# A four-layer graph and expert network: the first twelve expert slabs placed beside the last routing, a second table for the others, expert weights folded two by two, input variances on ScalarE

## The reference

```python
x = x + gnn0(layernorm(x), adj)      # 2-layer attention-like mixing with exp weights, per graph
x = x + ffn0(layernorm(x))           # 30 iterations: h += 0.01 tanh(h); silu; layernorm; h @ W + b
x = x + relu(f @ Gw[:128] + (adj @ f) @ Gw[128:] + bias),  f = layernorm(x)
# experts: 8 of them, the best 2 for each token
logits = xt @ Wr + br;  p = softmax(logits);  top_p, top_idx = top_k(p, 2);  w = top_p / sum(top_p)
xn = layernorm(xt)                                   # over 128 channels
h = gelu((xn * ln_g[e] + ln_b[e]) @ W1[e] + b1[e])   # 128 -> 512
y = h @ W2[e] + b2[e]                                # 512 -> 128
x = x + sum of w * y over the two chosen experts
```

## Time and profile before

| | |
|---|---|
| median of 3 runs | 2514.82 us |
| profiled execution | 2515.02 us, its span 2513.2 us |
| TensorE busy | 2373.5 us, 94% |
| VectorE busy | 2086.3 us, 83% |
| ScalarE busy | 1866.4 us, 74% |
| GpSimd busy | 2024.6 us, 81% |
| mean granted TensorE clock | 0.976 of 2.4 GHz |

### The profile page before, as it was taken

How to read it: one execution, slowest core, us unless ns; L and a number is a source line. 1 busy time by engine, 2 the same in 40 slices (tenths; PEclk the granted TensorE clock), 3 DMA queues, 4 the chain that set the end, 5 groups by cost and what they waited for, 6 DMA issues and landing times.

```text
span 2513.2 us, 61190 instructions
## 1 busy us (share of the span) xinstructions
PE 2373.5 (94%) x19694; PEld 2310.1 (92%) x19951; DVE 2086.3 (83%) x5808; ACT 1866.4 (74%) x2280; POOL 2024.6 (81%) x1733
## 2 busy tenths in 40 slices
PE   6929999999999999999999999999994999999998
PEld 6829999999999999999999999989973999999998
DVE  7999999999999999999999999998983444444443
ACT  3879999999999999999999999946531333333333
POOL 5879999999999999999999999995765444444444
PEclk9969999999999999999999999999986999999999
DMA  9200000000000000000000000011323655555554
GB/s 252 84 0 1 0 0 0 0 0 0 0 0 0 0 0 0 0 0 0 0 0 0 0 0 0 0 32 60 104 82 117 215 215 212 212 213 214 210 211 149
DMA packets 124120, 162.43 MB, mean 65 GB/s; under 512 B 14526, under 2 KB 77146, under 8 KB 124032
## 3 DMA queue, kind: packets, MB, share of 16 engines
q1 hardware_dynamic: 113792, 141.64, 16.9%
q0 software_dynamic: 9088, 17.14, 2.0%
q10 hardware_dynamic: 1152, 2.62, 0.3%
HBM read 36.35 MB, written 24.58 MB: 24 GB/s over the span
## 4 chain that ended last, share of the span: by engine, by line
DVE 59%; PE 31%; issue 6%; ACT 2%; POOL 1%; DMA 1%; SPq 0%; DVEq 0%; POOLq 0%; ACTq 0%
DVE pair_stats L605 26%; DVE state L689 20%; PE psum L1287 11%; PE psum L1296 11%; DVE state L670 7%; PE psum L1119 4%; PE psum L1109 2%; DVE it_vars L609 2%; DVE x_stats L605 1%; POOL sorted_rows L555 1%; ACT state L984 1%; PE psum L1246 1%; PE psum L1277 1%; DVE resid L716 1%; DVE state L685 1%
## 5 line engine op out<-in xcount | busy, mean ns | idle before, releaser
L1119 PEld LDWEIGHTS psum<-w_ffn,turned 128*128 128x128 f32 x7680 | 1009.4, 192 | 36.0
L1119 PE MATMUL psum<-w_ffn,turned 128*128 128x128 f32 x7680 | 1012.9, 275 | 12.8 <-issue 0.2
L510 POOL TENSOR_TENSOR it_rstd<-it_vars,minus_half 128x8 f32<-128x8 f32 x480 | 785.5, 1637 | 0.0
L513 POOL TENSOR_TENSOR state<-state,it_rstd 128x768 f32<-128x768 f32 x480 | 708.2, 1475 | 37.6
L605 DVE BATCH_NORM_STATS2 pair_stats<-state 128x6 f32<-128x256 f32 x1920 | 684.9, 416 | 0.0
L1109 PE MATMUL psum<-ident,state 128*128 128x128 f32 x4352 | 595.1, 280 | 55.9 <-DVE state L685 44.4
L689 DVE SCALAR_TENSOR_TENSOR state<-state,psum 128x1024 f32<-128x1024 f32 x464 | 560.3, 1208 | 0.2
L1109 PEld LDWEIGHTS psum<-ident,state 128*128 128x128 f32 x4352 | 476.3, 142 | 74.3 <-issue 56.7
L969 ACT COPY turned<-psum 128x1024 f32<-128x1024 f32 x480 | 485.8, 1012 | 78.4 <-PE psum L1109 40.8
L979 ACT ACTIVATE state<-state 128x1024 f32<-128x1024 f32 x480 | 512.8, 1068 | 29.3 <-DVE state L685 9.1
L976 ACT ACTIVATE state<-psum 128x1024 f32<-128x1024 f32 x464 | 480.9, 1036 | 0.0
(11 more groups left out here) (207 smaller groups left out, 1829.5 us busy)
## 6 DMA issues: line engine op xcount, KB each, us to landing
adjT<-resid SPq DMA_DIRECT2D x304, 320.0 KB, 2.4
adjT<-sorted_rows SPq DMA_DIRECT2D x156, 66.5 KB, 1.9
resid<-in_x_dram SPq DMA_DIRECT2D x16, 512.0 KB, 7.3
state<-in_adj_dram SPq DMA_DIRECT2D x16, 512.0 KB, 7.3
adjT_dram<-adjT SPq DMA_DIRECT2D x7, 512.0 KB, 4.9
adjT<-adjT_dram SPq DMA_DIRECT2D x7, 512.0 KB, 3.5
adjT<-resid ACTq DMA_DIRECT2D x8, 320.0 KB, 2.7
out_dram<-resid,store_at POOLq DMA_INDIRECT x156, 2.7
```

The source lines that it names most:

```text
L510: nc.gpsimd.tensor_tensor(it_rstd[s % 8][:, :], it_vars[s % 4][:, :], minus_half[:, 0:TILES], ALU.pow).then_inc(it_pow, 1)
L513: nc.gpsimd.tensor_tensor(values[s][:, 0:POOL_TILES, :], values[s][:, 0:POOL_TILES, :], wide(it_rstd[s % 8][:, 0:POOL_TILES]), ALU.mult).t ...
L1119: last = nc.tensor.matmul(dst[:, t, :], stationary(t), moving(t), start=bias is None and m == 0, stop=m == len(terms) - 1, skip_group_chec ...
```

## The change

- **Input variances.** In the last pass the sixteen variances of the input (L609 there) leave VectorE; ScalarE computes them as `x2_variance` with an Identity activation, scale 1/128 and a bias tile `offset`.
- **Folding.** The gain is put into the matrix as a diagonal: ScalarE builds `fold_mats` (ident times the gain plus the offset term), TensorE's product gives the whole folded matrix, ScalarE copies it back. Two experts are folded in each of slots 11 to 14, one ahead of the logits and one behind the ranks. The expert weights are loaded two by two, from the fifth stream on.
- **Twelve slabs first.** After six streams (EARLY = 5) at least 12 slabs are full whatever the input: (6 · 1024 - 28 · 127) / 128 = 20. At the end of slot 12 VectorE computes a table of these (`first_slabs`), in slot 14 it writes it (`first_table`). SyncE loads their rows from slot 14 on and their weights behind the folding, GpSimd scales all twelve with four instructions behind stream 9's scatters (`scale_first`). They have output tiles of their own (`y_first`), since their stores come only after the last scatter.
- **Loops shortened.** VectorE's slot loop ends with slot 18, TensorE's and ScalarE's with 19. What was left for the slots after is written out between the first slabs.
- **The others' table** is computed behind slabs 0 and 1, spread in two parts while TensorE is at slabs 4 and 5, and written behind slabs 3 and 4. Slabs 12 to 155 come out of it. The first round of twelve drains (`end=True`), and the turns of slabs 12 and 13 stand behind it.

```diff
+    EARLY = 5
...
-        FOLD_FROM = STREAMS - 3
+        FOLD_FROM = 11
+        TABLE_FROM = EARLY + PLACE_LAG
...
+            sp.wait_ge(tables_ready, 1)
+            for h in range(2):
+                sp.wait_ge(scattered[h], 16 * (EARLY + 1) * TILES // 2)
+            sp.wait_ge(mix_psum, 13)
+            for n in range(FIRST_ROWS):
+                load_rows(n)
+            second_weights(2)
+            sp.wait_ge(w1_scaled, NE)
+            sp.wait_ge(pads_b2_in, 16 * 3)
+            for n in range(2):
+                load_weights(n)
+            sp.wait_ge(x3_ready, 13)
+            second_weights(4)
+            for n in range(FIRST_ROWS, EACH):
+                load_rows(n)
+            sp.wait_ge(x3_ready, 14)
+            second_weights(6)
+            for n in range(2, 4):
+                load_weights(n)
+            for n in range(4, EACH):
+                load_weights(n)
             AHEAD = 3
-            sp.wait_ge(tables_ready, 1)
-            sp.wait_ge(pads_in, 16 * 2)
+            sp.wait_ge(tables_ready, 2)
+            load_weights(EACH)
             for h in range(2):
                 sp.wait_ge(scattered[h], 16 * STREAMS * TILES // 2)
-            for n in range(4 + AHEAD):
+            for n in range(EACH, EACH + AHEAD + 1):
                 load_rows(n)
...
+                if m == 9:
+                    for rows in row_groups:
+                        scale_first(rows, 0 if rows is row_groups[0] else FIRST_ROWS)
...
             for n in range(6):
-                scale(n)
-            for n in range(SLABS):
+                scale(EACH + n)
+                store(2 * n)
+                store(2 * n + 1)
+            for n in range(EACH, SLABS):
...
                         dve.wait_ge(x2_ready, k + 1)
+                        if k >= 4:
+                            dve.wait_ge(x2_var_ready, k - 3)
                         statistics(x1_stats[k % 4], resid[k]).then_inc(x2_stats_done, 1)
-                        dve.wait_ge(x2_stats_done, k + 1)
-                        variance(x_var[k], x1_stats[k % 4]).then_inc(x2_var_ready, 1)
...
+            def first_slab(o):
+                if o + 4 < EACH:
+                    normalize(0, o + 4)
+                finish(0, o)
+            last = STREAMS - 1
+            normalize(0, 0)
+            normalize(0, 1)
+            scale_logits(last - 1)
+            find_slots(last - 3)
+            route(last - 1)
+            rows_roots(last)
+            normalize(0, 2)
+            scale_logits(last)
+            find_slots(last - 2)
+            normalize(0, 3)
+            best(last, 0)
+            best(last, 1)
+            choose(last)
+            find_slots(last - 1)
+            find_slots(last)
+            first_slab(0)
+            other_slabs()
+            first_slab(1)
+            other_rows()
+            first_slab(2)
+            first_slab(3)
+            other_table(0)
+            first_slab(4)
+            other_table(1)
+            for o in range(5, EACH - 1):
+                first_slab(o)
...
+            def x2_variance(s):
+                act.wait_ge(x2_stats_done, s + 1)
+                nc.scalar.activation(halves(x_var[s]), of_stats(x1_stats[s % 4], 2), ACT.Identity, bias=offset[:, 0:1],
+                                     scale=1.0 / D).then_inc(x2_var_ready, 1)
...
+            def fold_matrix(e):
+                nc.scalar.activation(fold_mats[:, e, :], ident[:, :], ACT.Identity, bias=fold[:, e:e + 1],
+                                     scale=params[:, e, 0:1]).then_inc(fold_ready, 1)
+            def folded(e):
+                act.wait_ge(fold_psum, e + 1)
+                nc.scalar.copy(w1_all[:, e, 0:H], psW).then_inc(w1_scaled, 1)
...
-                if 0 <= k - FOLD_FROM < NE:
-                    fold_sums(k - FOLD_FROM)
+                if 0 <= k - FOLD_FROM < NE // 2:
+                    fold_sums(2 * (k - FOLD_FROM))
...
+                    ranks(h)
+                if 0 <= k - FOLD_FROM < NE // 2:
+                    fold_sums(2 * (k - FOLD_FROM) + 1)
...
+                    if first and o == 1:
+                        ranks(STREAMS - 2)
+                    if first and o == 3:
+                        ranks(STREAMS - 1)
+                    if first and o == 9:
+                        spread(psT[0], diag[0], "other")
+                    if first and o == 11:
+                        spread(psT[1], diag[1], "half")
```

More of the change, by code:

```diff
@@ new lines, in _, with count_slabs, sum_up @@
+            steps = pair_steps[:, 1, :]
+            def count_slabs(offset):
+                table(nc.vector.tensor_tensor(steps, pair_end[:, :], region_0[:, :], ALU.subtract))
+                table(nc.vector.tensor_scalar(steps, steps, 1.0 / SLAB, offset, ALU.mult, ALU.add))
+                table(nc.vector.tensor_scalar(steps, steps, float(1 << 23), None, ALU.add))
+            def sum_up():
+                reach, at = 1, 0
+                while reach < PAIRS:
+                    old, new = slab_ends[at], slab_ends[1 - at]
+                    table(nc.vector.tensor_tensor(new[:, LEAD:], old[:, LEAD:], old[:, LEAD - reach:LEAD + PAIRS - reach],
+                                                  ALU.add))
+                    reach, at = 2 * reach, 1 - at
+                assert at == 1
@@ L892, in _ @@
-            table(nc.vector.tensor_tensor(past[:, :, :], ends.unsqueeze(1).to_broadcast([P, 2, PAIRS]),
-                                          slab_j[:, :].unsqueeze(2).to_broadcast([P, 2, PAIRS]), ALU.is_le))
-            for h in range(2):
-                last = nc.vector.tensor_tensor(past_steps[:, h, :, :], pair_steps[:, :, :],
-                                               past[:, h, :].unsqueeze(1).to_broadcast([P, 5, PAIRS]), ALU.mult)
-            table(last)
-            table(nc.vector.tensor_reduce(slab_is[:, :, :], past_steps[:, :, :, :], AX.X, ALU.add))
@@ L944, in finish, with experts @@
                 last.then_inc(y_ready, 1)
-            def experts(i, first=False, end=False):
+            def first_slab(o):
[29 more added lines that the diff above has]
+                first_slab(o)
+            def experts(i, end=False):
                 for o in range(EACH):
@@ L950, in experts @@
                         normalize(i, o + 3)
-                    if not first or o >= 1:
-                        finish(i, o - 1, not first or o >= 5)
+                    finish(i, o - 1)
             for n in range(3):
-                normalize(0, n)
-            experts(0, first=True)
+                normalize(0, EACH + n)
             with dve.Fori(1, SLABS // EACH - 1, 1) as i:
@@ L1083, in experts @@
                     gelu(i, 2 * o + 1)
+                    if o in between:
+                        weights_exp(between[o])
             for n in range(2):
                 turn(0, n)
-            experts(0)
+            experts(0, end=True, between={0: STREAMS - 2, 1: STREAMS - 1})
+            for n in range(2):
+                turn(0, EACH + n)
             with act.Fori(1, SLABS // EACH - 1, 1) as i:
@@ L1311, in _ @@
             pe.wait_ge(experts_in[1], 16 * NE)
-            experts(0, first=True)
+            experts(0, first=True, end=True)
+            pe.wait_ge(tables_ready, 2)
+            for n in range(2):
+                turn(0, EACH + n)
             with pe.Fori(1, SLABS // EACH - 1, 1) as i:
```

402 lines of the change are left out of this document (250 added, 152 removed).

## The result

The changed kernel has a median of 2495.27 us over 4 runs (2492.36 to 2501.0); the kernel before, beside it, 2514.71 (4 runs, 2514.58 to 2514.89). The ratio is 0.9927 [0.9915, 0.994]: 19.4 us faster, where 27.5 were forecast. It spreads more than the kernel before, and its time goes with the mean granted clock of TensorE: 2492.36 at 0.981, 2501.0 at 0.977.

The account below looks back on a forecast made before the run. Bound: TensorE in the mixing layer, VectorE's routing from 1850, then GpSimd's scatters until 1921.5. Terms 32.3 - 1.2 - 2.6 - 1.0 = 27.5 us, off 2514.82, gave 2487.3; range 2478 to 2500.

Parts of the forecast that it names:

- Rivals 3 and 4: 3: VectorE stretches scatters of streams 11 to 15, slower, chance 0.05; 4: twelve slabs start late, 2514, chance 0.03.
- rival 1: Low clock in fold slots or slower scatters beside the experts take a third: gain 12 to 22, 2497, chance 0.28.
- that rival's clock term: TensorE's clock falls twice, not once, in each fold slot: 6.8 us of the gain lost.
- the signs that the prediction set: Slots 11 to 14 at 15 to 16 us each would be right; under 14.5 or over 17 wrong.
- Input variances: Moved from VectorE to ScalarE, the mixing layer's first copy starts 1.5 us earlier; bounds 0 and 12.
- Folds: Slots 11 to 14 on TensorE: eight pairs of products cost 16.0 us, low clock 1.7 once in each slot.
- Rival 2: The clock holds in the fold slots (+6.8): gain 34, 2480, chance 0.14.
- the working: From VectorE's slot 16 at 1851: first expert product 1888.8, slab 3's second product 1912.5, leaving 32.3 us.
- The seam: Behind slab 11: TensorE idle 2.6 us before slab 12, GpSimd's catching up 1.0 more; bounds 2 and 14.

Follow-up runs that it names:

- e3: The kernel before with only the input variances of the last iteration moved to ScalarE; ratio to the kernel before 1.0 [0.9985, 1.0015].
- e8: Same edit as e3, the kernel before with only the input variances on ScalarE, on another chip; ratio to the kernel before 0.9993 [0.9984, 1.0002].
- e10: The changed kernel with scatters begun only after the last mixing and each fold's bias product over 128 rows, not 8; 2586.55 us, one run.
- e5: The changed kernel again, unedited, on a chip where the kernel before took 2564.84 us; 2572.52 us, ratio to the kernel before 1.0026.
- e7: The changed kernel with GpSimd scaling slabs 12 to 15 ahead of its first stores; 2581.26 us, 8.7 us slower than e5 beside it.
- e12: The changed kernel with one fold in each of slots 11 to 18, not two in 11 to 14; 2486.45 us, ratio to the kernel before 0.9886.
- e9: The changed kernel with GpSimd's scatters begun only after VectorE's last mixing, bias product still 8 rows; 2601.18 us, one run.
- first trace of after: The first profiled execution of the changed kernel, unedited, on the first chip; 2494.73 us.

## Why the prediction was right, and where its size was off

**The bound was right.** The time came from the hole between the last mixing products and 1928.46, VectorE's routing let TensorE begin, and GpSimd's scatters, with 0.95 us each, let it go on. Rivals 3 and 4 did not happen: no scatter stretched to 2.1 us, the first slabs did start. The gain, 19.4 us, lies where rival 1 had it (12 to 22), and that rival's clock term (6.8 us there, 5.1 measured) is most of what took it. By the signs that the prediction set, the folds were wrong: slots 11 to 14 were to last 15 to 16 us, and under 14.5 or over 17 was to count against it; they last 14.03, 15.47, 17.94 and 17.48.

**Input variances:** 1.5 us forecast. One takes 0.30 us on ScalarE, not 0.2, and the first copy came 2.3 us earlier (1694.80), but of the gain behind it nothing is shown: the 1.0 us at slot 11 is within the difference of one execution from another, and e3 and e8 can't tell 1 us from none.

**Folds, the mis-sized term.** The step said "1.7 once in each of four slots; bounds 0 and 3.4 a slot". The trace has 0, 3.4, 3.4 and 5.1, together 11.9 instead of 6.8. The one low stretch behind a fold in the earlier trace rows was taken as one price a slot, though a second pair now stood inside it. The pairs themselves were 16.0 forecast and 16.5 measured. Up to VectorE's slot 16 this is nearly the whole delay of 6.1 us (forecast 1851, measured 1857.10): 5.1 for the clock, 0.5 for the pairs and 0.3 because slot 11 began at 1781.50 and not at 1781.2. The forecast took the fall as given by the narrow products of logits and ranks; e10 shows that in this kernel the 8 rows of the bias product decide, and that with 128 no low clock is left in these slots. It is a cost that the kernel before already paid once a fold. Rival 2 counted on the 512 columns of the second pair to hold the clock; they did not.

**From there the working held:** first product 6.3 us late (1895.09 against 1888.8), of which 6.1 came in with slot 16; slab 3's second product 3.8 late (1916.34 against 1912.5), since the waits behind it were 2.5 us shorter than forecast. Those 2.5 us are luck: they hid a part of the error of the folds.

**The seam:** a gap of 3.6 us, not 2.6, and slab 12's first product 5.5 late (1950.35 against 1944.8). The stores and scalings alternate as forecast (1945.35 to 1949.52), and GpSimd took 3.1 us to scale the twelve slabs, as forecast; it came to them 7 us late by the folds, and its six streams took 64.0 us and not 63.1. The gap is followed by a stretch of low clock (0.50 and 0.82 in the windows from 1952 and 1954), which costs 1.7 us and was not in the sum. That makes the 7.0 us by which the spans' difference (20.5) falls short of 27.5: 3.8 from the folds, 1.7 from the seam, and 1.5 more than forecast behind it, which the low clock covers.

**What the prediction didn't see** is that its profile showed one chip. The ratio is 0.9927 on the first and 1.0026 on the chip of e5. The gaps and waits beside dense indirect transfers of GpSimd fit both: the change puts expert work beside the scatters. e7 adds to that by making the stores dense, and gets new gaps. That is argued, not shown. Why the engines wait there stays open: the profile names no releaser, and the scatters were never taken away on such a chip.

## What to carry to other kernels

Where TensorE sets the pace, look at the granted clock behind each product that fills few rows; letting it run over 128 rows, of which the other operand's zeros cancel all but one, cost no time here and kept the clock at 1.00 (e10, one trace, without scatters beside it). Put extra TensorE work where another engine is the bound, even if each piece is as dear: with four folds moved behind slot 14 the kernel took 8.8 us less (e12). A gain from running one stage beside another is measured on more than one chip, with the kernel before beside it on each.

## What had not been expected of the hardware

- A TensorE busy 16.00 of 16 us was granted 0.79 with a bias product of 8 rows (e9) and 1.00 with 128 rows (e10), the rest of the code the same.
- The same two programs took 2514 and 2495 us on one chip and 2565 and 2573 us on another. Loops ran alike there (from 600 to 1100 us ScalarE is busy 478.93 us in the first trace of after and 478.96 in e5), and so did the expert slabs from 2100 to 2300 (TensorE 199.99 us of 200 in both, clock 1.00). In between ScalarE and VectorE waited 149 us in e5 for something that the profile doesn't name, and 0 in the first trace.
- Eight indirect stores 1.27 us apart were followed by gaps of 0.8 to 1.7 us on TensorE (e7); with 1.3 and 1.9 us between them in turn there was one of 1.3 us beside the first two stores, and none of over 0.3 behind it (e5).
